# An expert layer whose rows are gathered through a slot-to-token map, and whose results are combined in one stretch

## The reference, cut to what matters

```
logits = tokens @ wg                            # 4096 x 8
idx1, idx2 = the two largest; g1, g2 = softmax gates, normalised to g1 + g2
loc1 = cumsum(mask1) - mask1                    # place of a token in its expert's queue
loc2 = cumsum(mask2) - mask2 + sum(mask1)
keep = loc < C                                  # C = 1024 slots per expert
disp[idx * C + min(loc, C - 1)] += tokens * keep      # both choices: 8192 slots x 256
eo = gelu(disp @ w_gate) @ w_down               # for each of 8 experts, inner width 1024
out = g1 * keep1 * eo[f1] + g2 * keep2 * eo[f2]
x = layernorm(x + out)
```

## Time and profile before

| | us |
|---|---|
| runs: median of 3 (lowest, highest) | 10040.86 (10026.58, 10059.51) |
| profiled execution, its own time | 10058.28 |
| its span in the trace | 10056.5 |
| expert layer within the span, from the last instruction of the layer before (1606.7) to its own last (2438.4) | 831.7 |
| TensorE busy in the whole span | 8297.1 (83%) |

### The profile page before, as it was taken

How to read it: one execution, slowest core, us unless ns; L and a number is a source line. 1 busy time by engine, 2 the same in 40 slices (tenths; PEclk the granted TensorE clock), 3 DMA queues, 4 the chain that set the end, 5 groups by cost and what they waited for, 6 DMA issues and landing times. The chain is left out here.

```text
span 10056.5 us, 125255 instructions
## 1 busy us (share of the span) xinstructions
PE 8297.1 (83%) x45414; PEld 4713.3 (47%) x45414; DVE 5780.4 (57%) x10917; ACT 4316.8 (43%) x7413; POOL 2031.4 (20%) x1790
## 2 busy tenths in 40 slices
PE   4878575794798988998999698888888689989998
PEld 1222144463233335654664354445434344458888
DVE  6777442003676755643662488776554365657776
ACT  3666331111355555632651367665222144444443
POOL 1111111103011101100110044334000011127775
PEclk8888765896899988999999799889988789989999
DMA  3222141121222110000000000000000123336665
GB/s 69 42 42 42 23 80 67 53 71 48 35 43 42 31 18 20 2 4 20 1 4 0 14 1 1 1 1 3 9 6 1 23 47 53 57 111 195 195 197 174
DMA packets 223368, 463.98 MB, mean 46 GB/s; under 512 B 50987, under 2 KB 90774, under 8 KB 220984
## 3 DMA queue, kind: packets, MB, share of 16 engines
q1 hardware_dynamic: 155175, 240.91, 11.8%
q0 software_dynamic: 67584, 215.02, 7.3%
HBM read 366.63 MB, written 75.53 MB: 44 GB/s over the span
## 5 line engine op out<-in xcount | busy, mean ns | idle before, releaser
L819 ACT ACTIVATE probs<-scores 128x1024 f32<-128x1024 f32 (+4 forms) x960 | 868.1, 937 | 888.5 <-PE scores L696 629.3
L908 DVE TENSOR_REDUCE row_max<-ring 128x1 f32<-128x512 f32 (+3 forms) x1792 | 1024.8, 625 | 250.3 <-PE ring L670 223.5
L696 PE MATMUL scores<-query_stack,key_stack 99*128 99x512 bf16 (+3 forms) x2816 | 850.0, 393 | 167.1 <-DVE levels L930 77.5
L3858 POOL DMA_INDIRECT r_got<-in_L_ffn_tables,r_index x768 | 779.5, 1015 | 457.2 <-DVE r_index L4154 203.7
L716 PE MATMUL outputs<-probs,head_values 128*32 128x512 f32 (+3 forms) x5632 | 782.3, 630 | 102.7 <-ACT probs L816 100.0
L816 ACT ACTIVATE probs<-levels,quant 128x1024 f32<-128x1024 uint8 x512 | 612.7, 1233 | 327.7 <-DVE levels L930 325.0
L930 DVE TENSOR_SCALAR levels<-scores 128x1024 uint8<-128x1024 f32 x512 | 607.5, 1219 | 178.4 <-PE scores L696 146.3
L670 PE MATMUL ring<-key_stack,query_stack 96*128 96x512 bf16 (+3 forms) x1792 | 607.2, 381 | 62.9 <-DMA key_stack<-normed_parts 40.1
L3676 DVE TENSOR_TENSOR_SCAN ssm_pre<-ssm_pre,added 128x1024 f32<-128x1024 f32 x256 | 571.0, 2270 | 33.0 <-ACT ssm_pre L3634 33.0
L696 PEld LDWEIGHTS scores<-query_stack,key_stack 99*128 99x128 bf16 x2816 | 257.5, 104 | 690.1 <-DVE levels L930 276.5
L3611 PE MATMUL state_sums<-term,constants 128*128 128x512 f32 x1024 | 494.8, 606 | 43.6 <-POOL term L3642 34.5
(11 more groups left out here) (669 smaller groups left out, 16111.6 us busy)
## 6 DMA issues: line engine op xcount, KB each, us to landing
joined_heads<-heads_out SPq DMA_DIRECT2D x512, 32.0 KB, 2.0
expert_w<-in_L_ffn_w SPq DMA_DIRECT2D x16, 1024.0 KB, 11.5
quant_parts<-parts SPq DMA_DIRECT2D x48, 256.0 KB, 5.0
query_stack<-quant_parts SPq DMA_DIRECT2D x48, 256.0 KB, 8.4
key_stack<-quant_parts SPq DMA_DIRECT2D x48, 256.0 KB, 8.3
query_stack<-cross_parts SPq DMA_DIRECT2D x48, 256.0 KB
normed_parts<-parts SPq DMA_DIRECT2D x48, 256.0 KB, 5.1
query_stack<-normed_parts SPq DMA_DIRECT2D x48, 256.0 KB, 8.6
```

Source lines behind the costliest of these rows:

```text
L696: last = nc.tensor.matmul(out[:, off:GROUP], keys, q_stack[0:rows, h, half * GROUP + off:(half + 1) * GROUP], start=True, stop=not edge)
L819: nc.scalar.activation(dst, s_ps[0:k_rows, 2 * (e % 2):2 * (e % 2) + 2, off:GROUP], ACT.Exp, scale=scale).then_inc(probs_ready, 1)
L908: nc.vector.reduce_max(row_max[:, i, qt, at:at + 1], src[:, 0:cols], AX.X).then_inc(ring_read, 1)
L3858: nc.gpsimd.indirect_dma_start(out=got[:, k % GOT_ROWS, :], out_offset=None, in_=io["L3_ffn_tables"], in_offset=bass.IndirectOffsetOnAxis( ...
```

## The change

- `token_rows` is one step without a loop. It also loads the gate weights, clears 4 KB per partition of zeros and issues all transfers: the weights of expert 0 first, then after each group the store of its rows into a DRAM tensor `stored_rows`, then the weights of expert 1, then 16 writes of zeros over `produced`. TensorE reads the residual itself; ScalarE and VectorE take turns in copying pairs of tiles out of PSUM.
- `route` no longer makes `place` and `scatter_to`. It makes a map from each of the 8192 slots to its token by one-hot marks: in eight chunks of 8 tiles VectorE makes `tile_hot` (two instructions) and `at_hot` (one), and TensorE sums the products over all tokens in PSUM. From the sums come `source` (the row to fetch for a slot; 0 for an empty one) and `target` (token + 4096 x choice; out of bounds for an empty one).
- The step with the 64 scatters into `dispatched` is gone. In the experts' step GpSimd gathers each tile of 128 slots from `stored_rows` by `source` and scatters each finished tile of `made` to `produced` by `target`. SP only fetches weights.
- `combine` fetches `produced` by 16 plain transfers and runs all eight groups in one step, in one order written out for all engines: for each s the scaling of group s - 2, centring, squares, variance, root, inverse and spreading of group s - 1, and weighing, mixing, turning, sum and mean of group s. The first weighing is moved from VectorE to ScalarE.

```diff
@@ token_rows @@
+        turn_ps = ctx.enter_context(banks(nc, "rows_psum", [P, 4, GROUP], F32))
+        pairs = TOKEN_TILES // 2
+            def _(pool):
+                nc.gpsimd.memset(zeros[:, :], 0.0).then_inc(cleared, 1)
+            def _(sp):
+                sp.dma_start(gate_w[:, :, :], io["L0_ffn_wg"].rearrange("(c p) e -> p c e", p=P)).then_inc(gate_loaded, 16)
+                fetch_weights(sp, 0)
+                for g in range(GROUPS):
+                    sp.wait_ge(act_copied, g + 1)
+                    sp.wait_ge(dve_copied, g + 1)
+                    sp.dma_start(stored_rows[g * GROUP:(g + 1) * GROUP, :].rearrange("(t p) d -> p t d", p=P), rows[:, g * per:(g + 1) * per, :]).then_inc(rows_stored, 16)
+                fetch_weights(sp, 1)
+                sp.wait_ge(cleared, 1)
+                for n in range(whole.shape[0]):
+                    sp.dma_start(whole[n], zeros[:, :]).then_inc(zeroed, 16)
+            def _(pe):
+                for i in range(pairs):
+                    if i >= 4:
+                        pe.wait_ge(copied[i % 2], i // 2 - 1)
+                    for t in (2 * i, 2 * i + 1):
+                        for c in range(FC):
+                            at = t % 2 * DIM + c * P
+                            last = nc.tensor.transpose(turn_ps[:, i % 4, at:at + P], chip.xt[:, c, t * P:(t + 1) * P], chip.c(C_ID))
+                    last.then_inc(turned, 1)
+                    if i == 0:
+                        pe.wait_ge(gate_loaded, 16)
+                    for t in (2 * i, 2 * i + 1):
+                        for c in range(FC):
+                            last = nc.tensor.matmul(logit_ps[:, t, :], chip.xt[:, c, t * P:(t + 1) * P], gate_w[:, c, :], start=(c == 0), stop=(c == FC - 1))
...
@@ route @@
-                then(nc.vector.tensor_copy(place[:, :, :], slot[:, :, :]))
-
-                then(ts(index[:, :, :], keep[:, :, :], -float(2 * EXPERTS * CAPACITY), float(2 * EXPERTS * CAPACITY), ALU.mult, ALU.add))
-                then(tt(slot[:, :, :], slot[:, :, :], index[:, :, :], ALU.add))
-                then(nc.vector.tensor_copy(scatter_to[:, :, :], slot[:, :, :]))
+                then(ts(high[:, :, :], slot[:, :, :], 1.0 / P, 0.5 / P - 0.5, ALU.mult, ALU.add))
+                then(ts(high[:, :, :], high[:, :, :], ROUND, ROUND, ALU.add, ALU.subtract))
+                then(nc.vector.scalar_tensor_tensor(out=slot[:, :, :], in0=high[:, :, :], scalar=-float(P), in1=slot[:, :, :], op0=ALU.mult, op1=ALU.add))
+                for k in range(2):
+                    then(ts(token[:, k, :], chip.c(C_IOTA, N), float(P), chip.c(C_LANE, 1), ALU.mult, ALU.add))
+                    if k:
+                        then(ts(token[:, k, :], token[:, k, :], float(TOKENS), None, ALU.add))
+                then(tt(token[:, :, :], token[:, :, :], keep[:, :, :], ALU.mult))
+                for m, (k, n) in enumerate(chunks):
+                    if m >= 2:
+                        dve.wait_ge(marks_used, m - 1)
...
+                    then(tt(tile_hot[:, m % 2, :, :], own(high, SLOT_TILES), line(SLOT_TILES), ALU.is_equal))
+                    then(tt(tile_hot[:, m % 2, :, :], tile_hot[:, m % 2, :, :], own(token, SLOT_TILES), ALU.mult))
+                    tt(at_hot[:, m % 2, :, :], own(slot, P), line(P), ALU.is_equal).then_inc(marks_ready, 1)
...
+                for m in range(len(chunks)):
+                    pe.wait_ge(marks_ready, m + 1)
+                    for n in range(MAP_TILES):
+                        last = nc.tensor.matmul(map_ps[:, :], at_hot[:, m % 2, n, :], tile_hot[:, m % 2, n, :],
+                                                start=(m == 0 and n == 0), stop=(m == len(chunks) - 1 and n == MAP_TILES - 1))
+                    last.then_inc(marks_used, 1)
@@ experts @@
+                for e in range(2, EXPERTS):
+                    sp.wait_ge(y_ready, tiles * (e - 1))
+                    fetch_weights(sp, e)
...
+                def take(e):
+                    if e >= 2:
+                        pool.wait_ge(turned, FC * parts * (e - 1))
+                    for t in range(tiles):
+                        nc.gpsimd.indirect_dma_start(out=taken[:, e % 2, t, :], out_offset=None, in_=stored_rows,
+                                                     in_offset=bass.IndirectOffsetOnAxis(ap=source[:, e * tiles + t:e * tiles + t + 1], axis=0)).then_inc(arrived[e % 2][t // per], 16)
+
+                pool.wait_ge(rows_stored, 16 * GROUPS)
+                take(0)
+                take(1)
+                pool.wait_ge(zeroed, all_zeroed)
+                for e in every:
+                    for t in range(tiles):
+                        pool.wait_ge(made_ready, e * tiles + t + 1)
+                        nc.gpsimd.indirect_dma_start(out=produced, out_offset=bass.IndirectOffsetOnAxis(ap=target[:, e * tiles + t:e * tiles + t + 1], axis=0),
+                                                     in_=made[:, e % 2, t, :], in_offset=None, bounds_check=2 * TOKENS - 1, oob_is_err=False).then_inc(scattered[e % 2], 16)
+                    if e + 2 < EXPERTS:
+                        take(e + 2)
@@ combine @@
+        order = []
+        for s in range(GROUPS + 2):
+            order += [(kind, s - lag) for kind, lag in (("scale", 2), ("centre", 1), ("squares", 1), ("weigh", 0), ("mix", 0), ("turn", 0), ("var", 1), ("sum", 0), ("root", 1), ("inverse", 1), ("mean", 0), ("spread", 1))
+                      if 0 <= s - lag < GROUPS]
...
+                for g in range(GROUPS):
+                    for k in range(2):
+                        start = k * TOKENS + g * GROUP
+                        sp.dma_start(got[:, g, k, :, :], produced[start:start + GROUP, :].rearrange("(t p) d -> p t d", p=P)).then_inc(fetched[g], 16)
```

More of the change, by code:

```diff
@@ new lines, in _ @@
+                turn(0)
+                for g, (e, j) in enumerate(groups):
+                    if j == parts - 1 and e + 1 < EXPERTS:
+                        turn(e + 1)
+                    if e >= 2 and j == 0:
+                        dve.wait_ge(scattered[e % 2], 16 * tiles * (e // 2))
+                    for m in range(g * per, (g + 1) * per):
+                        dve.wait_ge(y_ready, m + 1)
+                        nc.vector.tensor_copy(made[:, e % 2, m % tiles, :], y_ps[:, m % 2, 0:DIM]).then_inc(made_ready, 1)
```

444 lines of the change are left out of this document (232 added, 212 removed).

## The result

The changed kernel takes **9957.8 us**, the median of four runs (9955.2 to 9963.3), against 10048.5 us for the kernel before in as many (10026.6 to 10059.5): a ratio of 0.9914 with a 95% interval of 0.9901 to 0.9927, or 73 to 99 us less. The gain is real, and two thirds to three quarters of the forecast one: the range of 9866 to 9968 holds it, the forecast case's own range (9885 to 9945) does not. The execution that the profiler recorded took 9957.5 us, its span 9955.7.

A forecast was written before the change was run, and what follows sets the result against it. Some 350 us of the 831.7 us layer lie outside TensorE-bound experts, with nothing hidden. Terms -39 + 28.5 - 84 - 0.6 - 34.5 = -130 us gave 9928 against the profiled execution, 9911 against the median; range 9866 to 9968.

The forecast's parts named there:

- the forecast case: Whole kernel: the prediction's own account holds, 9911 us with own range 9885 to 9945; chance 0.58.
- the largest term: Scatter and start of the experts, route's end to first multiplication: 84 us less, ends 80 and 86.
- SP's queue: Token rows: the barrier waits for SP's issues, ending 21.5 us after TensorE, so route begins at 1657.
- I take it cold for the first 4 to 5 us and warm after that, 25 us: Token rows: TensorE soon reaches 2.4 GHz because it is no longer interrupted, and ends at 1635.
- it would alternate: Map: TensorE switches between cold (31 us) and warm (23.5 us) over the eight chunks; 27 us taken.
- half way: Combining: 110 us, between 127 cold and 93 warm, so 34.5 us less.
- the clock decides: Rival: TensorE stays at 1.2 GHz in token rows, map and combining, whose pipeline is a chain; 9950 to 9959 us; chance 0.17.
- Has landed 2.9 us after that: Start of the experts: the eighth gather lands 2.9 us after its issue, within 16.5 us to the first multiplication.
- the cover in the experts: Experts: one scatter and eight gathers take 14.4 us, needed only after 27.5 us, leaving 13 us to spare.
- the experts cost nothing more: Experts' stretch: no change in time from its 468.6 us, though GpSimd issues 16 transfers per expert.
- the last scatter, 0.6 us less: End of the experts: last scatter, 1.0 + 2.9 us and the barrier, against 5.3 us before.
- The slower rival: Experts: GpSimd's queue sets the pace and TensorE waits; slower than before from an issue of 5.7 us; chance 0.02.

The follow-up runs named there:

- fillers: Changed kernel plus idle 512-column f32 matmuls per token-row pair, per map chunk and before each combining turn: layer 714.9 us against 720.2, whole 10254.1 us.
- combine_front: Changed kernel with combining's order rewritten: weigh, mix, turn first, then centre and squares, then scale: combining 67.9 us against 120.7, whole 10235.8 us.
- scale_late: Changed kernel with only the scaling of group s - 2 moved behind the turning of group s: combining 99.5 us against 120.7, whole 10330.6 us.
- adjacent_rows: Changed kernel with every gather taking 128 neighbouring rows, output not the reference's: start 15.3 us against 19.3, whole 10292.6 us.

## Why the prediction was right or wrong

**Right: the direction, the place and the mechanism of the largest term.** Most of the gain is the scatter that went: its stretch gives 81.4 us, where the layer as a whole gives 110.9. Nothing hides outside the layer, and what was saved arrived at the end but for what the unchanged layers took. The eighth gather was issued 8.92 us behind the first (1721.78 and 1730.70), 8.9 as worked out. The map's three VectorE instructions took 0.69, 0.69 and 1.23 us against 0.68, 0.68 and 1.21. ScalarE loads a function table once in the whole combining. That the time lies in the range owes something to luck: the 8.0 us of the experts, which the prediction had at nothing, and the 5.7 us by which SP's queue was quicker made up for part of what the clock cost. Without those 13.7 us it would be 9971, above the range.

**Wrong: the clock**, the step "I take it cold for the first 4 to 5 us and warm after that, 25 us". The prediction reasoned that the pauses of before held the clock down and would go. They went, TensorE was busy for 35 us without a gap, and the clock stayed at 0.50. The 4 to 5 us come from no row; in fillers, where the clock did rise, it took some 13 us of unbroken work. It is that one misreading three times:
- Token rows: TensorE ended at 1648.3, not 1635, so 13.3 us late. SP's last issue, put 21.5 us behind that, came 15.8 behind it, with no issue of the zeros above 1.7 us. Together 7 us short. The forecast of the stretch came close by two errors against one another.
- Map: TensorE's 8 chunks at 3.41 us are the cold case (8 x 3.5), not "it would alternate". With VectorE's first chunk ahead they take 30.3 us (1687.54 to 1717.85), where the prediction took 27 and had 31 as its cold end. Route is 4 us short, 3.3 of them here.
- Combining: 120.7, between the half way of 110 and the cold end of 127. 10.6 us short. Here "the clock falls after each pause of TensorE and comes back late" was right, and half way was too hopeful: a mean of 0.61 with a round of 13.7 to 14.3 us against 15.2 cold and 10.8 warm.

The time is that of the rival "the clock decides" (9950 to 9959, 0.17), and so is the mechanism in its first two places. In the third the rival said the pipeline is a chain in fact, which combine_front and scale_late show. The Trainium skill says (TensorE: Matmul & The Clock Gate, Part 1: The HAM clock gate) that activity releases TensorE's throttle. Here it stayed at 1.2 GHz through 35 us of unbroken work on records of 128 and of 8 columns, and the measurement decides.

**Wrong: the landing.** "Has landed 2.9 us after that" took the landing of `got`, the nearest row there was; the eighth gather of scattered rows was waited for until 6.8 us after its issue began (1730.70 to 1737.47). A window in the middle of the gathers of `got` shows the difference, a DMA share of 0.46 for 111 GB/s where the changed kernel has 0.86 for 82:

```profile
2300.00:2303.00 3.00, 0.00 (x0) 0.00 (x0) 0.00 (x0) 0.00 (x0) 2.39 (x3) 0.50 0.46 111
```

That is 3.9 us too little, and 1.2 us of it came back since transposes and copy took 1.8 us and not 3.0. adjacent_rows, whose eighth gather was waited for 2.7 us, has the start at 15.3 us. The median landing, 4.1 us, did no harm later: the cover in the experts held, and no expert after the first waited for `taken`.

**Wrong: "the experts cost nothing more"** in the good direction. The reordered transposes took away a wait that the kernel before had at the experts. The 6.3 us of idle time in its group were there to be read (the earlier trace rows has one such wait, 0.78 us on `taken_t`), and the prediction named that part of the order only for its cost at the start.

**Wrong: "the last scatter, 0.6 us less"**. It was 1.7 more: from the last made copy to the combining are 7.0 us, of which the issue is 0.98 and the rest landing and barrier.

**The slower rival and the trap.** An issue of GpSimd had a median of 947 ns and a longest of 1110 beside VectorE's work, far from the 5.7 us at which the rival began, and in line with the earlier trace rows. The Trainium skill has a transfer of GpSimd's queue take 3100 ns beside a VectorE copy (SBUF — State Buffer, A bandwidth-pool intuition that's wrong, on the "DVE blocks DMA" trap). The longest issue in the changed kernel's profile is 1998 ns, in the last layer. VectorE's copies in this stretch read PSUM, so the trace doesn't test that rule in its own conditions.

## What to carry to other kernels

Price TensorE by form and by the clock that the profile shows for that form in company like the new one, not by how busy it will be; removing its pauses did not raise the clock of the token rows or the map. In a pipelined order written out by hand, put what later engines wait for first, and read from the trace who stands idle ahead of which step: one line of order was worth 53 us here, half as much as the whole change. Behind a barrier, count the queue that issues, since 16 writes of a DMA queue were 14.5 us of tail that the next step could hide.

## What the runs showed of the hardware that was not expected

- TensorE stayed at 1.2 GHz for 35 us while busy throughout with 128- and 8-column f32 records, and for 25 us in the map. With two 512-column f32 records added per pair or chunk it came to 2.4 GHz after 12 to 13 us of unbroken work and stayed there; with one 512-column bf16 record it did not in a window of 36 us.
- Gathers of 128 rows of 1 KB kept the DMA engines at a share of 0.86 for 82 GB/s where the rows were scattered, and at 0.35 for 96 GB/s where they were neighbours (0.40 and 0.15 us a packet). Rows some 8 KB and some 256 KB apart were alike.
- Sixteen plain writes issued in a row took SP 0.9 us each on average and 1.7 at the longest, where the kernel before had one issue stand for 15.4 us.
- The unchanged linear attention takes 573 to 574 us in some profiles and 583 to 593 in others, with mean clocks of 0.80 to 0.81 and 0.77 to 0.79.
- The kernel before, unchanged, had its combining at 143.8 us in one profile and 155.2 in another, on another chip, with ScalarE waiting 11 to 12 us in each looped round.
